# A fast-weight attention layer with 32 routed experts on one core: experts over all tokens in place, against rows sorted by expert group

## The reference

```python
A = X @ X.transpose(0, 2, 1)
B = b * A + c * (A @ A)
X = a * X + B @ X
```

```python
group_scores = jax.lax.top_k(grp, 2)[0].sum(-1)
_, gidx = jax.lax.top_k(group_scores, TOPK_G)
...
_, topi = jax.lax.top_k(masked, TOP_K)
...
x_lat = x @ fc1_w.T
h = relu2(jnp.einsum('tl,eil->eti', x_lat, w1))
h = h * cw.T[:, :, None]
y_lat = jnp.einsum('eti,eli->tl', h, w2)
routed = y_lat @ fc2_w.T
```

## Time and profile before

| | |
|---|---|
| median of 3 runs | 831.35 us (829.08 to 831.86) |
| the profiled execution | 830.14 us |
| its span, first to last instruction | 828.1 us |
| granted TensorE clock | 0.996 of full speed |
| length of a full body (stage 0 to stage 0), 14 of them | 51.3 us |

### The profile page before, as it was taken

One profiled execution on the slowest core, in us unless ns is written; L12 is line 12 of the kernel. 1 busy time (PEld: TensorE's weight loads), 2 busy tenths in 40 slices (PEclk: granted clock), 3 DMA queues, 4 the chain that ended last, 5 costly groups with the idle time before them and its releaser, 6 DMA issues.

```text
span 828.1 us, 24889 instructions
## 1 busy us (share of the span) xinstructions
PE 780.7 (94%) x9776; PEld 668.5 (81%) x9776; DVE 714.6 (86%) x2592; ACT 354.0 (43%) x868; POOL 406.8 (49%) x535
## 2 busy tenths in 40 slices
PE   3899999999999999999999999999999999999997
PEld 1888888888888888878888788887888888888886
DVE  4789898898988979889798897988979889898876
ACT  2544344443444434444344444444444444434533
POOL 1654555445454454544555445544465444655442
PEclk9899999999999999999999999999999999999999
DMA  8100000000000000000000000000000000000000
GB/s 321 54 3 14 9 2 21 3 13 9 2 21 2 14 8 2 21 2 15 8 3 20 2 15 9 3 21 2 15 8 2 21 2 15 8 2 15 2 15 7
DMA packets 9811, 15.09 MB, mean 18 GB/s; under 512 B 1120, under 2 KB 8928, under 8 KB 9440
## 3 DMA queue, kind: packets, MB, share of 16 engines
q1 hardware_dynamic: 7904, 7.80, 3.2%
q10 hardware_dynamic: 1792, 5.70, 1.8%
HBM read 11.41 MB, written 2.10 MB: 16 GB/s over the span
## 4 chain that ended last, share of the span: by engine, by line
PE 53%; DVE 33%; issue 6%; ACT 5%; POOL 2%; DMA 1%; SPq 0%; DVEq 0%
PE CC L629 18%; PE M L629 13%; PE HB L629 8%; DVE acc L1328 8%; PE YB L629 8%; DVE Wn L1175 4%; DVE Mp L1138 2%; DVE dhb L1094 2%; DVE X L1146 2%; PE CC L699 2%; DVE Am L1131 2%; POOL r L285 2%; DVE sm L1233 1%; DMA rows<-in_rows 1%; PE CC L700 1%
## 5 line engine op out<-in xcount | busy, mean ns | idle before, releaser
L363 POOL TENSOR_TENSOR hq<-hr 128x512 f32<-128x512 f32 x128 | 137.1, 1071 | 71.9 <-ACT hr L426 71.9
L285 POOL TENSOR_TENSOR r<-r,half 128x3 f32<-128x3 f32 (+1 forms) x78 | 77.9, 1011 | 155.1 <-DVE r L1116 67.9
L629 PE MATMUL HB<-xlT,e_s 128*128 128x128 f32 x1024 | 143.0, 283 | 0.4 <-ACT xlT L426 0.4
L629 PE MATMUL YB<-e_s,hq 128*128 128x128 f32 x1024 | 141.3, 281 | 1.8 <-DVE acc L1328 0.8
L629 PEld LDWEIGHTS HB<-xlT,e_s 128*128 128x128 f32 x1024 | 126.7, 193 | 6.8 <-ACT xlT L426 0.7
L1328 DVE SCALAR_TENSOR_TENSOR acc<-YB,cw,acc 128x128 f32<-128x128 f32 x448 | 125.4, 342 | 7.9 <-PE YB L629 7.9
L341 POOL TENSOR_TENSOR aX<-X,a_tile 128x192 f32<-128x192 f32 x150 | 92.9, 640 | 79.9 <-DVE X L1146 79.9
L426 ACT ACTIVATE hr<-HB 128x512 f32<-128x512 f32 x128 | 76.1, 594 | 128.5 <-PE HB L629 128.5
L629 PEld LDWEIGHTS YB<-e_s,hq 128*128 128x128 f32 x1024 | 124.2, 191 | 7.4 <-issue 4.1
L629 PEld LDWEIGHTS CC<-X,Mp 64*64 64x64 f32 x1800 | 58.3, 135 | 23.6 <-issue 11.3
L629 PEld LDWEIGHTS CC<-Am 64*64 64x64 f32 x1800 | 59.5, 134 | 21.8 <-DVE Am L1131 18.2
(11 more groups left out here) (180 smaller groups left out, 1525.3 us busy)
## 6 DMA issues: line engine op xcount, KB each, us to landing
xa<-in_x SPq DMA_DIRECT2D x16, 128.0 KB, 2.1
e_s<-in_e1T ACTq DMA_DIRECT2D x1, 2048.0 KB, 12.7
e_s<-in_e2T ACTq DMA_DIRECT2D x1, 2048.0 KB, 19.3
xr<-in_x SPq DMA_DIRECT2D x16, 128.0 KB, 2.2
out<-ot SPq DMA_DIRECT2D x16, 128.0 KB, 1.7
wall<-in_wall SPq DMA_DIRECT2D x1, 820.0 KB, 7.1
up_s<-in_upT ACTq DMA_DIRECT2D x1, 512.0 KB, 15.9
down_s<-in_downT ACTq DMA_DIRECT2D x1, 512.0 KB, 20.0
```

The lines of the kernel that those rows point to most:

```text
L285: return pool.tensor_tensor(dst, src, expo[:, 0:n], ALU.pow)
L363: pool.tensor_tensor(hq[b][:, :, :], hr[b][:, :, :], hr[b][:, :, :], ALU.mult).then_inc(e_hq, 1)
L629: return pe.matmul(out_, lhsT, rhs, start=start, stop=stop)
```

## The change

The experts are taken out of the tiles. The layer norm of all 16 tiles, their fc1 and their gate logits are computed ahead, in the start and in bodies 0 and 1 (`ln_turned`, `gate_rows` on TensorE, `ln_xnT`, `ln_apply`, `gate_out` on ScalarE). In body 1 one routing over all 2048 tokens runs on VectorE in 46 steps, one behind each instruction of a head pair: `group_best` to `chosen` pick groups and experts, `totals` to `group_base` count the tokens of each group and lay the groups out in 35 tiles of 128 rows (`NJ` = 35), `rank` to `indices` give each token two row numbers, and the last seven steps give the weights.

In bodies 2 and 3 GpSimd writes each token's x_lat and eight weights to its two rows in DRAM with 32 indirect DMAs (`scatter`). In bodies 4 to 13 each of the 35 row tiles passes through the eight experts of its group in two units of four: 70 units, 7 a body (`PER` = 7), in place of 128. The weights are now multiplied into the hidden layer by VectorE (`h_weight`, one instruction of 512 elements a unit), ScalarE does relu and square, and the eight experts of a tile are summed in one PSUM group, copied and stored (`keep`). For each row tile SyncE loads its group's two expert tables (512 KB each), its rows, and its weights once more as a broadcast over partitions (512 KB), into a ring of three. GpSimd fetches the two result rows of each token with 32 indirect DMAs (`gather`), 17 in body 14 and 15 in the last body, and the output of all tiles is then finished in eight pairs: sum, turn, fc2, add, store (`last_sum`, `last_turn`, `last_yT`, `last_fc2`, `last_out`).

The core of the diff:

```diff
-NU = E // EU
+ROW = P + EPG
+RING = 3
+HALVES = EPG // EU
+PER = 7
+FIRST = 4 * PER
...
+    NJ = 2 * NT + NG - 1
+    UNITS = NJ * HALVES
+    SORT_STEP, SCAT_STEP = 1, 2
+    xs_d = nc.dram_tensor("sorted_rows", [NJ * P, ROW], F32)
+    cw_d = nc.dram_tensor("tile_weights", [NJ, P * EPG], F32)
+    y_d = nc.dram_tensor("sorted_out", [NJ * P, P], F32)
...
+        def h_unit(i, k):
+
+            n = PER * i + k - FIRST
+            return n if 0 <= n < UNITS else None
...
+        def y_unit(i, k):
+
+            n = PER * i + k - FIRST - 2
+            return n if 0 <= n < UNITS else None
+
+        def turn_tile(i, k):
+
+            n = PER * i + k - FIRST - 2
+            j = 0 if n == -2 else (n + 3) // 2 if n >= -1 and n % 2 else NJ
+            return j if j < NJ else None
...
+            def load(j):
+                b = j % RING
+                if j >= RING:
+                    sp.wait_ge(e_y, HALVES * (j - RING + 1))
+                else:
+                    sp.wait_ge(e_rt, RT_OWNERS)
+                    sp.wait_ge(e_zeroed, 16 * 5)
+                first = sp.value_load(owner_i[0:1, j:j + 1], min_val=0, max_val=E - EPG)
+                sp.dma_start(e1_s[b][:, :, :], e1T[:, bass.ds(first, EPG), :]).then_inc(e_tile[b], 16)
+                sp.dma_start(e2_s[b][:, :, :], e2T[:, bass.ds(first, EPG), :]).then_inc(e_tile[b], 16)
+
+            def gather_rows(j):
+                b = j % RING
+                if j == 0:
+                    sp.wait_ge(e_scat, 16 * 2 * NT)
+                sp.dma_start(xs[b][:, :], xs_d[j * P:(j + 1) * P, :]).then_inc(e_rows[b], 16)
+
+            def spread(j):
+                b, n = j % RING, j // RING
+                sp.wait_ge(e_rows[b], 16 * (n + 1))
+                sp.dma_start(cw_d[j, :].rearrange("(p e) -> p e", p=P), xs[b][:, P:ROW]).then_inc(e_gate[b], 16)
+                sp.wait_ge(e_gate[b], 32 * n + 16)
+                sp.dma_start(cwb[b][:, :], cw_d[j, :].partition_broadcast(P)).then_inc(e_gate[b], 16)
+
+            def keep(j):
+                sp.wait_ge(e_yo, j + 1)
+                sp.dma_start(y_d[j * P:(j + 1) * P, :], yo[j % 2][:, :]).then_inc(e_ysto[j % 2], 16)
+
+            for j in range(RING):
+                load(j)
+            for j in range(RING):
+                gather_rows(j)
+                spread(j)
+            for j in range(RING, NJ):
+                keep(j - RING)
+                load(j)
+                gather_rows(j)
+                spread(j)
+            for j in range(NJ - RING, NJ):
+                keep(j)
...
+            def scatter(n):
+
+                t, j = n // 2, n % 2
+                if n == 0:
+                    pool.wait_ge(e_rt, RT_ALL)
+                    pool.wait_ge(e_gl, NT // 2)
+                    pool.wait_ge(e_zeroed, 16 * 5)
+                pool.indirect_dma_start(
+                    xs_d[:, :], bass.IndirectOffsetOnAxis(ap=dest_i[:, t, j:j + 1], axis=0),
+                    xsrc[:, t, j, :], None).then_inc(e_scat, 16)
...
+                if n == 0:
+                    for b in range(2):
+                        pool.wait_ge(e_ysto[b], 16 * ((NJ + 1 - b) // 2))
+                pool.indirect_dma_start(
+                    xsrc[:, t, j, 0:P], None, y_d[:, :],
+                    bass.IndirectOffsetOnAxis(ap=dest_i[:, t, j:j + 1], axis=0)).then_inc(e_gat[t // 8], 16)
...
+                    if (SCAT_STEP, 6) <= (i, st) and moved:
+                        if i > 5:
+                            if (i, st) >= GATHER_AT:
+                                moved.pop(0)()
+                        elif len(moved) > 2 * NT:
+                            moved.pop(0)()
...
+            GATHER_AT = (14, 3)
+            moved = [lambda n=n: scatter(n) for n in range(2 * NT)] + [lambda n=n: gather(n) for n in range(2 * NT)]
...
+            def h_relu(i, k):
+                n = h_unit(i, k)
+                if n is None:
+                    return
+                b = n % RING
+                act.wait_ge(e_h, n + 1)
+                if n >= RING:
+                    act.wait_ge(e_y, n - RING + 1)
+                flat = hb[b][:, :, :].rearrange("p s t -> p (s t)")
+                a(flat, HB[:, :], ACT.Relu).then_inc(e_hs, 1)
+                act.wait_ge(e_hs, 2 * n + 1)
+                a(flat, flat, ACT.Square).then_inc(e_hs, 1)
...
                     for f in fill.get(st, []):
                         f()
-                h_up(m, 0)
+                y_slot(i, 6)
                 out_wo(i)
-                turn_y(i, False)
-                h_up(m, 1)
+                h_slot(i, 6)
                 turn_w(m, 0)
-                out_fc2(i)
                 turn_w(m, 1)
...
+            def h_weight(i, k):
+
+                n = h_unit(i, k)
+                if n is None:
+                    return
+                j, b = n // HALVES, n // HALVES % RING
+                dve.wait_ge(e_hs, 2 * n + 2)
+                if n % HALVES == 0:
+                    dve.wait_ge(e_gate[b], 32 * (j // RING + 1))
+                c = n % HALVES * EU
+                gate = cwb[b][:, :].rearrange("p (t e) -> p e t", e=EPG)[:, c:c + EU, :]
+                nc.vector.tensor_tensor(hb[n % RING][:, :, :], hb[n % RING][:, :, :], gate, ALU.mult).then_inc(e_hw, 1)
...
+            def last_sum(n):
+                if n % 4 == 0:
+                    dve.wait_ge(e_gat[n // 4], 16 * 16)
+                dve.wait_ge(e_yt, n)
+                nc.vector.tensor_tensor(ys[:, :, :], xsrc[:, 2 * n:2 * n + 2, 0, 0:P], xsrc[:, 2 * n:2 * n + 2, 1, 0:P], ALU.add)\
+                    .then_inc(e_ys, 1)
...
-                        if st > 10 and routing:
+                        if routing and (i, st) >= (SORT_STEP, 1):
                             routing.pop(0)()
                     for f in fill.get(st, []):
                         f()
                 update(i)
-                y_sum(i)
+                h_weight(i, 6)
                 renorm(m)
                 w_bd(m)
                 total(i)
...
+                rest = [group_best(0), group_best(1), group_best(2), group_best(3), group_sum, beaten, group_wins, selected, penalty, masked,
+                        best(0), best(1), best_marked(0), best_marked(1), best_marked(2), best_marked(3), chosen,
+                        totals, doubling(0), doubling(1), doubling(2), doubling(3), enough, group_tiles,
+                        group_end(0), group_end(1), group_end(2), group_end(3), owners, owner_sum, owner_row, group_base,
+                        rank, placed, own, high, low, indices,```

`h_unit` and `y_unit` say which unit stands at place k of body i: the y side is two places behind the h side. `turn_tile` places the turning of row tile j by TensorE behind the y block of the same place.

Where instructions move, three places matter. The first is VectorE's list at the end of a body, between `update` and `renorm`. Before:

```order
L1156 TENSOR_REDUCE r<-sq 128x3 x2
L1333 TENSOR_TENSOR ya<-acc 128x256
L1335 TENSOR_TENSOR ys<-ya 128x128
L1170 TENSOR_SCALAR r<-r 128x3
L1172 RECIPROCAL r<-r 128x3
L1175 TENSOR_SCALAR Wn<-Wn,r,nrm 128x64 x3
```

More of the change, by code:

```diff
@@ L30 @@
 F32 = mybir.dt.float32
+I32 = mybir.dt.int32
+U32 = mybir.dt.uint32
 AX_X = mybir.AxisListType.X
@@ new lines, in extra, with last_turn @@
+            def extra(i, k, half):
+                n = ln_turn(i, k, half)
+                if n is not None:
+                    ln_turned(n)
+                n = gate_pair(i, k, half)
+                if n is not None:
+                    gate_rows(n)
+            def last_turn(n):
+                pe.wait_ge(e_ys, n + 1)
+                pe.wait_ge(e_yT, n)
+                for l in range(2):
+                    ins = pe.transpose(HB[:, l * P:(l + 1) * P], ys[:, l, :], ident[:, :])
+                ins.then_inc(e_yt, 1)
```

814 lines of the change are left out of this document (486 added, 328 removed).

## The result

The changed kernel takes 862.6 us (median of 859.73 to 863.52), the kernel before 830.81 us beside it: ratio 1.038, 95% interval 1.035 to 1.041. Slower, as forecast, but by 31.8 us where the sum gave 9.7; that is 3.8%, outside the forecast's own range of 834 to 856 us and in the part above 3% that had a chance of 0.15. The profiled execution spans 861.7 us against 828.1.

The account below looks back on a forecast made before the run. No engine alone was taken as the bound: TensorE and VectorE hand the chain to each other. The terms sum to +9.7 us on 830.14, 839.8, or 841 as a median; own range 834 to 856, 8 in 10 within 808 to 870.

Parts of the forecast that it names:

- Bodies 4 to 13: Ten bodies with units: net +0.7 us each, with the body 4 and late-row corrections +7.5 us in all.
- That is 3.35 us later: End of a unit body: VectorE starts scaling at 438.5 instead of 435.15, behind the seventh unit's h_weight.
- -1.05, -0.75, -0.85: Gains per unit body: rounds shorter by 1.05 us, three scalings no longer held 0.75, dhb not held 0.85.
- the 2 us for late rows: Bodies 4 to 13: a tile's rows may load late at every second body's third place, 2 us in all.
- the 1.5 us taken off for body 4: Body 4 has no down blocks at first, so it was counted 1.5 us shorter.
- A body without units saves 7.4 us: Bodies 2, 3 and most of 14: rounds fall 6.1 us to 28.8, the head phase gains the rest.
- c = 1.05 us: GpSimd's time for one indirect DMA in bodies 2, 3, 14 and the last, taken as 1.05 us.
- Body 14 and the last: End of the kernel: body 14 at -7 + 3.7 us, the last body +6.2 us at 34.5, priced by its gathers.
- Body 1 and the start: Start +1 us; body 1 +7 us, from 38 routing steps run on VectorE between the stages.
- 1: Freeing VectorE from GpSimd's locks shortens each of 14 bodies by 1.8 us more: 803 to 816 us, chance 0.32.
- rival 2: Still slower: c 1.5 us or more (870 us), or SyncE's loads late in ten bodies (871 us); chance 0.15.
- 3: TensorE is the bound and its removed work counts in full: 713 us; chance 0.03, with anything far below.

Follow-up runs that it names:

- e9: Changed kernel with four useless matmuls ahead of the turn of the new weights in bodies 4 to 13, seventh h_weight left in place: 869.8 us.
- e5: Changed kernel with the seventh h_weight behind total, plus four useless matmuls at each of 14 expert-block places in bodies 1, 2, 3, 14: 815.8 us.
- e7: Changed kernel with the seventh h_weight later, body 14's last gathers behind the roots, eight gathers ahead of the last body's shared square: 809.8 us.
- e8: e7 plus two output pairs between steps of the last attention, the others through two banks and four output buffers: 806.4 us, 804.5 when repeated.
- e4: Changed kernel with all 64 indirect DMAs left out, tiles holding zeros: 843.2 us.
- e10: Changed kernel with the seventh h_weight later, plus eight GpSimd squares of 128 x 512 a body in bodies 4 to 13: 858.5 us.
- f3: Changed kernel with each of the 64 indirect DMAs replaced by a GpSimd square of 128 x 600: 865.4 us.
- e12: e8 plus seven useless blocks in each of bodies 1, 2, 3, 14, three in the last body, and last sums waiting in lots: 824.5 us.
- g1: Changed kernel with only the seventh h_weight moved behind total, a repeat run: 834.4 us.

## Why the prediction missed the size

The direction was right, and the wait that makes the unit bodies longer. Three steps of the sum failed: the clock behind a wait of TensorE was put at nothing, a body without units was taken to get shorter than its chain does, and the last body was priced by its gathers, with its attention chain well under them. In the prediction's terms:

- **Bodies 4 to 13 (+7.5 forecast, +17.1 measured).** The step that ends in "That is 3.35 us later" was right in size (3.3 us by e9 against e5, e7, e8). Missing is the clock: 1.3 us a body, 13 in all (e9). The text expected the clock to fall only in the last wait of the program. The rest of the difference has the other sign: all other terms together (-1.05, -0.75, -0.85) came to -2.65 a body and measured -2.95, the 2 us for late rows were not needed (TensorE waited 0.2 us for xs in all), and the 1.5 us taken off for body 4 did not come (it took 53.4 us like the others).
- **"A body without units saves 7.4 us".** It saves 4.65 (e4). The rounds were taken to fall to 28.8 us; the runs show the body's length and not which stages stay longer. Over bodies 2 and 3 this is 3 us too much gain, the leftover routing steps (eight of the 46) counted in.
- **c = 1.05 us.** The instruction was near (0.97), the pitch is 1.25: the sum took the length of an instruction where it needed the time from one to the next. By the formulas of the text with 1.25 bodies 2 and 3 cost 10.5 us for the 4.1 taken; 8.7 were measured (102.2 against e4's 93.5), mostly as waits for roots and not for aX.
- **Body 14 and the last (+2.9 forecast, +15.7 measured).** Body 14 took 42.99 us, 0.3 less than before and not 3.3. The last took 44.25 for 34.5: 10.65 and not 7 until the root, at the low clock; 15 gathers 18.8 and not 15.75; and 12.7 and not 9.7 behind them, of which 2.2 are a wait of the last output buffer for the store of the one two back. But the rows were waited for 0.87 us only: the attention chain, taken as 14 us, took 23.5, most of it at the low clock, and with four pairs behind it is nearly as long as the gathers. e4, with no gathers at all, still needs 79.8 us for the stretch, against 71.6: eight serial pairs behind the attention are a cost of their own.
- **Body 1 and the start** came out 5.8 us better than taken.
- **Rivals.** 1 names a real mechanism (e10), but the 1.8 us a body beyond what was priced did not come; that e8's 804.5 us lies in its range of 803 to 816 is luck, as e8 changes the wait and the end. The time fell where rival 2 put it (above 3%), and that too is luck: c was not 1.5 or more, and SyncE's loads were not late (TensorE waited 0.2 us for rows in all). 3 (TensorE as the bound) is refuted by the result itself: TensorE's busy time fell by 53.5 us and the time rose.
- **The two pages.** The Trainium skill (Perfetto Trace Analysis, Identifying the Most-Contended Engine) tells one to optimize the engine with the highest occupancy first, though it would judge TensorE's headroom by its weight loads (81% here) and not by its matmuls (94%). Relieving that engine brought nothing here. The Trainium skill (SBUF — State Buffer, SBUF: two separate sides) has a DMA issued by GpSimd go from 620 to 3100 ns beside a two-port step of VectorE. No run here shows that: the indirect DMAs take GpSimd 0.97 us in the median with and without gaps, 1.42 at most in the traces of the changed kernel. Whether the gaps have to do with it no run tells.

What is left open: what the gaps are. They come only where GpSimd issues indirect DMAs, and with a series: three had them, two and the first comparison had not, and one chip had a series of each kind, so the chip is not it either. Leaving the DMAs out (e4) is all that was seen to remove them in a series that had them; f3 was not run in such a series, and the trace names no releaser.

The version that beats both kernels is e8: 804.5 us beside 830.2 (ratio 0.9705, interval 0.969 to 0.972) in a series without gaps. It was not run in one with gaps; e12, close to it, was, and had 821 to 825.

## What to carry to other kernels

When work of a full engine is cut out, ask at each wait that is left what the engine's clock does behind it: here 3.3 us of waiting cost 4.6. An instruction that gates a weight for later must not stand in the queue ahead of the one that the critical chain waits for; moving one line was worth 46 us in 880. And for a queue of equal instructions read the time from start to start, never the duration alone.

## What the runs showed of the hardware

- TensorE's granted clock fell to its lower level in or behind waits of 3.5 and 5.6 us (444.3 and 812.9 in the changed kernel). In the ten unit bodies it came back some 3 to 7 us later; in the thin last body it was low for 24 us of the next 27.
- An indirect DMA of 128 rows keeps GpSimd for 0.97 us and the next starts 1.25 us after it; a gather's rows land 2.5 us after issue.
- Squares of GpSimd of 128 x 512 elements, eight in a unit body, raise VectorE's busy time there from 39.4 to 42.2 us for the same instructions (g1, e10).
- A VectorE product of 128 x 512 with one operand read at every eighth element takes 1178 ns, contiguous 775.
- In some series, starts of VectorE, ScalarE and TensorE come late by 1 to 4 us, at times more, in the bodies where GpSimd issues indirect DMAs, 17 us in this kernel (880.5 against 863.3); in others they never do.
